# Second loop's front computed one round ahead; three convolution blocks split over ScalarE and GpSimd

## The chip, the cores and the metric

One core of one Trainium2 chip. The time is the device time of one launch in microseconds, the median of the runs shown. The kernel is written engine by engine: TensorE (PE), VectorE (DVE), ScalarE (ACT), GpSimd (POOL) and SyncE (SP, which issues the DMAs) each have an instruction stream of their own, in order, and meet only at semaphores.

## The reference

Two layers over 8 sequences of 512 tokens with 128 features. Layer 0 (attention and 32 experts) is the first loop and is not touched. Layer 1, for each sequence:

```python
xn = layernorm(x)                                  # the outer normalisation, eps 1e-5
z  = zrms(xn, w_ln1)                               # x * rsqrt(mean(x*x)) * (1 + w)
q, k, v, gate = split(z @ W_qkvz); b, a = split(z @ W_ba)
beta = sigmoid(b); g = -exp(A_log) * softplus(a + dt_bias)
q, k, v = split(silu(causal_dwconv(concat[q, k, v], conv_w)))   # 4 taps, each channel by itself
core = gated_delta_rule(l2norm(q), l2norm(k), v, g, beta)       # chunks of 128 tokens
h = xn + (rms(core) * silu(gate)) @ W_out;  x2 = zrms(h, w_ln2)
a1 = h + moe(x2; 8 experts of 64, top 2)
a2 = ffn(xn; 8 experts of 512, top 2, gelu, router xn @ w_router)
out = x + a1 + a2
```

## The kernel before

Both layers are hardware loops of 8 rounds (`Fori(0, LOOPS)`, one per engine), one round per sequence. The order of the work in a round of the second loop is written out by hand in `schedule_l1` (L132 to L175) as a list of steps; every engine walks through the same list and issues its own part of each step, so a step that stands earlier in the list is ahead of all later ones in the queue of each engine that has a part in it.

Each round of the second loop begins with a *front* that is not in the list and stands at the head of the loop's body. DVE: statistics of `x1` (L1189 to L1194), `xn1` (L1431), its mean square (`ms`, L1408 to L1411), `zz` (L1437), the router's shift (L1414, L1415), `zT` (L1441), then beta, the parts of the gate `sp` and the router's top 2 (L1445 to L1453). POOL: two powers (L1122, L1124). PE: `xn1` transposed (L654), the router's product (L665), `zz` transposed, the product with `Wba` (L674). ACT: the copy `xn1T` (L979), three exponentials (L981 to L985), a logarithm (L987). `x1` for the next round is loaded by SP late in the round before (L442).

After the front comes the convolution. Its 24 blocks of 128 channels go two at a time: `qkv` (PE, L682, block m into PSUM bank 2 + m % 4; ACT, L994, writes the last tap, block times weight, to `CV`), `taps` (DVE, L1478: three scaled additions per block, read from the bank, added into `CV`), `silu` (ACT, L1001). Blocks 0 to 7 are queries and keys and also go through a square (ACT, L1006) and a sum of squares on PE (`ssq`, L708, read by `stat`, DVE L1495); blocks 8 to 15 are values. Between the two halves lie the decay matrices `Gam` (scans on DVE L1490, ACT L1013, POOL L1137) and the products of keys (`prep`, PE L721, DVE L1521). The pieces of the last feed-forward (`ffn(n)`: `fh` on PE L859, gelu on ACT L1078, `fo` on PE L869) are strewn between the steps. After the values come `wfT` (DVE L1467), `cz` (PE L729, waits for `wfT` because it uses the same bank), the substitution (DVE L1534, L1536) and the chunks. The round ends with h1 to h5 (the second normalisation and the router of the small experts), `facc` 7 and the four pairs of small experts `moe1` (PE L909, L911, L915, L903; ACT L1089; DVE L1688, L1692) and the last addition `moe1_last` (DVE L1698), which raises `out_ready`.

The lines of the value half's order:

```python
order += [("scan", 1), ("gam",), ("prep", 0), ("prep", 1), ("qkv", 8), ("prep", 2), ("prep", 3), ("rr",), ("qkv", 10)]
order += [("taps", 8)] + ffn(2) + [("taps", 10)] + ffn(2) + [("silu", 8), ("qkv", 12), ("taps", 12), ("silu", 10), ("qkv", 14)]
order += [("taps", 14), ("silu", 12), ("wfT",), ("silu", 14), ("cz", 0), ("cz", 1), ("stat2",), ("cv", 0), ("sub", 0)]
```

## Time and profile before

| | |
|---|---|
| median of 3 runs | 3202.34 us (3197.88 to 3214.34) |
| the profiled execution | 3201.73 us, its span 3199.9 us |
| PE / DVE / ACT / POOL busy in the span | 2706.7 / 2034.1 / 1180.9 / 380.0 us |
| mean granted TensorE clock | 0.88 |
| chain that ended last | PE 52%, issue 27%, DVE 9%, DMA 4%, ACT 4% |

The second loop takes the last 2020 us of the span. In a timeline row the columns are start, busy time, engine, line, operation, output<-input, shapes and count; in brackets how long the engine was idle before it and for whom. Rows that merge several instructions give the time from the first to the last.

### The profile page before, as it was taken

What the parts mean: (1) busy time and instruction counts of PE and PEld (TensorE: products, weight loads), DVE (VectorE), ACT (ScalarE), POOL (GpSimd) and SP (SyncE); (2) the same over time, 40 slices, a digit from 0 to 9 for tenths busy, and PEclk for the clock granted to TensorE, in tenths of its full rate; (3) what the DMA queues carried; (4) which work ended last, traced back from release to release, by engine and by line L of the source; (5) the groups of instructions that cost most, each with busy time, mean ns of one, the idle gap of its engine ahead of it and who ended that gap; (6) DMA issues with size and microseconds to landing.
All of it is one profiled execution on the core that took longest, in us unless ns stands there. A gap on an engine that the chain in (4) does not pass through costs nothing.

```text
span 3199.9 us, 48490 instructions
## 1 busy us (share of the span) xinstructions
PE 2706.7 (85%) x14996; PEld 1821.9 (57%) x14996; DVE 2034.1 (64%) x6290; ACT 1180.9 (37%) x2164; POOL 380.0 (12%) x282
## 2 busy tenths in 40 slices
PE   2888888888888867987997997897898798798799
PEld 1434344343443425864874684685596495586487
DVE  4757567575665858458557657557656755845855
ACT  0132231322313234435444444444444444443543
POOL 0000000000000002112112112021120220211211
PEclk9888889898898967997997997997998899799799
DMA  4010201202012021101101101101201201110110
GB/s 137 9 37 11 27 17 21 37 7 32 13 26 37 2 50 53 34 28 40 47 11 57 47 11 53 51 8 47 60 1 54 53 8 40 41 34 28 47 40 14
DMA packets 133704, 109.69 MB, mean 34 GB/s; under 512 B 76968, under 2 KB 117488, under 8 KB 132944
## 3 DMA queue, kind: packets, MB, share of 16 engines
q1 hardware_dynamic: 130192, 100.01, 12.5%
q10 hardware_dynamic: 3264, 6.82, 0.6%
q8 instruction: 100, 1.64, 0.2%
q14 instruction: 148, 1.21, 0.1%
HBM read 86.62 MB, written 20.19 MB: 33 GB/s over the span
## 4 chain that ended last, share of the span: by engine, by line
PE 52%; issue 27%; DVE 9%; DMA 4%; ACT 4%; SPq 2%; POOL 2%; DVEq 0%; ACTq 0%; POOLq 0%
PE bank L859 5%; PE bank L869 4%; PE bank L654 4%; DMA arena<-scrk 3%; PE bank L708 2%; PE bank L729 2%; PE bank L553 2%; PE bank L608 2%; PE bank L811 2%; PE bank L769 2%; PE bank L774 2%; PE bank L757 2%; DVE arena L1478 2%; PE bank L761 2%; PE bank L682 2%
## 5 line engine op out<-in xcount | busy, mean ns | idle before, releaser
L869 PEld LDWEIGHTS bank<-wring,arena 128*128 128x128 f32 x2048 | 272.1, 194 | 118.8 <-issue 117.6
L859 PE MATMUL bank<-arena,wring 128*128 128x512 f32 x512 | 286.2, 641 | 41.2 <-ACT arena L1078 41.2
L1078 ACT ACTIVATE arena<-bank,w_b 128x512 f32<-128x512 f32 x256 | 175.9, 687 | 309.7 <-PE bank L859 309.4
L1478 DVE SCALAR_TENSOR_TENSOR arena<-bank,w_convw,arena 128x511 f32<-128x511 f32 (+2 forms) x384 | 255.1, 734 | 43.1 <-ACT arena L994 42.8
L869 PE MATMUL bank<-wring,arena 128*128 128x128 f32 x2048 | 274.0, 278 | 0.0
L960 ACT ACTIVATE arena<-bank 128x512 f32<-128x512 f32 x136 | 81.2, 597 | 501.3 <-PE bank L538 427.4
L1343 DVE CUSTOM_DVE_ANT_0 bank<-bank,arena 128x128 f32<-128x128 f32 (+3 forms) x512 | 248.9, 492 | 0.0
L969 ACT ACTIVATE arena<-bank 128x512 f32<-128x512 f32 (+1 forms) x384 | 171.1, 536 | 147.0 <-PE bank L595 145.5
L654 PE MATMUL bank<-w_ident,arena 128*128 128x128 f32 (+2 forms) x1032 | 147.6, 284 | 64.0 <-DVE arena L1431 62.1
L568 PE MATMUL bank<-arena 48*128 48x128 bf16 (+3 forms) x512 | 111.2, 319 | 69.0 <-DVE arena L1343 35.7
L1046 ACT ACTIVATE arena<-bank 128x512 f32<-128x512 f32 (+1 forms) x256 | 118.5, 487 | 135.5 <-PE bank L769 69.5
L654 PEld LDWEIGHTS bank<-w_ident,arena 128*128 128x128 f32 (+2 forms) x1032 | 121.2, 143 | 81.4 <-DVE arena L1431 63.8
L538 PE MATMUL bank<-arena 128*128 128x512 f32 x272 | 157.8, 664 | 7.8 <-ACT arena L960 7.8
L553 PE MATMUL bank<-arena 128*128 128x128 f32 x1088 | 161.8, 293 | 2.7 <-DVE arena L1328 2.7
L1643 DVE SCALAR_TENSOR_TENSOR arena<-bank,arena 128x128 f32<-128x128 f32 x224 | 63.0, 344 | 154.2 <-PE bank L869 152.4
L324 DVE TENSOR_TENSOR tick<-nhalf 128x1 f32<-128x1 f32 x597 | 93.2, 156 | 99.1 <-PE bank L568 92.5
L682 PE MATMUL bank<-arena,w_Wqkvz 128*128 128x512 f32 x256 | 151.4, 734 | 1.3 <-DVE arena L1478 1.3
L541 PE MATMUL bank<-arena 128*128 128x512 f32 x272 | 152.0, 643 | 0.0
L568 PEld LDWEIGHTS bank<-arena 48*128 48x128 bf16 x512 | 34.1, 93 | 204.6 <-DVE arena L1343 92.6
L553 PEld LDWEIGHTS bank<-arena 128*128 128x128 f32 x1088 | 135.7, 196 | 22.7 <-issue 11.7
L1147 POOL TENSOR_TENSOR arena<-arena,w_blk 128x512 f32<-128x512 f32 x64 | 79.7, 1266 | 555.8 <-PE bank L757 358.7
L729 PE MATMUL bank<-w_Wqkvz,arena 128*128 128x512 f32 x128 | 82.5, 794 | 61.7 <-DVE arena L1467 61.1
(275 smaller groups left out, 5271.5 us busy)
## 6 DMA issues: line engine op xcount, KB each, us to landing
wring<-in_w_last SPq DMA_DIRECT2D x64, 512.0 KB, 3.3
arena<-scrg SPq DMA_DIRECT2D x32, 512.0 KB, 5.4
arena<-scrq SPq DMA_DIRECT2D x108, 64.0 KB
arena<-scrk SPq DMA_DIRECT2D x108, 64.0 KB
scrn<-arena SPq DMA_DIRECT2D x64, 64.0 KB, 1.9
arena<-scrn SPq DMA_DIRECT2D x8, 512.0 KB, 3.5
scrx<-arena SPq DMA_DIRECT2D x8, 512.0 KB, 2.6
arena<-scrx SPq DMA_DIRECT2D x64, 64.0 KB, 2.1
```

The costliest lines, as they stand in the source:

```text
L538: mm(bk[:, :], W["gate0"][:, p, :] if p < PR0 else W["sg"][:], xnT, start=True, stop=True).then_inc(*s["p_gate"].up)
L541: mm(bk[:, :], W["up0"][:, p, :] if p < PR0 else W["su"][:], xnT, start=True, stop=True).then_inc(*s["p_up"].up)
L553: last = mm(bank[7][:, t * P:(t + 1) * P], HID[:, p % 2, t * P:(t + 1) * P], W["down0"][:, p, :] if p < PR0 else W["sd"][:], start=(p == 0 ...
L654: return nc.tensor.transpose(dst, src, W["ident"][0:k, 0:k])
L682: mm(bk[:, :], W["Wqkvz"][:, m * P:(m + 1) * P], zT, start=True, stop=True).then_inc(*s["p_qkv"].up)
L729: mm(bk[:, :], zT[:, c * P:(c + 1) * P], W["Wqkvz"][:, w:w + 4 * P], start=True, stop=True).then_inc(*s["p_z"].up)
L859: mm(bank[HBANK[e]][:, :], wring[:, e % 2, k * P:(k + 1) * P], xn1T, start=True, stop=True).then_inc(*s["p_fh"].up)
L869: last = mm(bank[OBANK[e]][:, t * P:(t + 1) * P], GH[:, f % 2, t * P:(t + 1) * P], wring[:, e % 2, FC * P + k * D:FC * P + (k + 1) * D], s ...
L969: fn(PT[:, slot, col:col + w], bank[SBANK[n % 4]][:, 0:w], ACT.Exp, scale=float(HD) ** -0.5).then_inc(*s["a_p"].up)
L1078: fn(GH[:, f % 2, :], bank[HBANK[f // FC]][:, :], ACT.Gelu_apprx_tanh, bias=W["b1"][:, f:f + 1]).then_inc(*s["a_gh"].up)
L1343: v.tensor_tensor_reduce(bk[:, 0:w], bk[:, 0:w], W["maskq"][:, S - w:S], 1.0, PAD, ALU.add, ALU.max, mx[:, col:col + 1]).then_inc(*s["v_ma ...
L1478: ins = v.scalar_tensor_tensor(out=cv[:, k:S], in0=bank[2 + m % 4][:, 0:S - k], scalar=W["convw"][:, m, 3 - k:4 - k], in1=cv[:, k:S], op0= ...
```

## The change

The front is taken out of the loop's head. One copy of it runs ahead of the loop for sequence 0 (`ahead_of_loop`); in the loop it becomes steps of the list that compute the next sequence's front: `gn` behind `h4`, `gx` behind `facc` 7, and `gT`, `gz`, `gr`, `gzT`, `gba`, `gend` among and behind the four `moe1`. Its PSUM results now all lie in bank 0. The last round computes a front that nobody reads. Three blocks of values (9, 11, 13) lose their three DVE taps: ACT writes block times weight into a buffer (`A[0]` or `A[1]` in turn) and POOL adds it into `CV`; the third of each block waits until POOL has freed the first buffer. Whoever waited for `v_cv` of such a block now waits for `g_tap` (`convolved`).

```diff
+POOLED = (9, 11, 13)
...
+def convolved(m):
+
+    return ("g_tap", 3 * POOLED.index(m) + 3) if m in POOLED else ("v_cv", m + 1 - sum(p < m for p in POOLED))
...
-    order += [("h2",), ("facc", 6), ("h3",)] + ffn(1) + [("h4",)] + ffn(2) + ffn_rest() + [("h5",), ("facc", 7)]
-    order += [("moe1", p) for p in range(PR1)] + [("moe1_last",)]
+    order += [("h2",), ("facc", 6), ("h3",)] + ffn(1) + [("h4",), ("gn",)] + ffn(2) + ffn_rest() + [("h5",), ("facc", 7), ("gx",)]
+    order += [("moe1", 0), ("gT",), ("gz",), ("moe1", 1), ("gr",), ("moe1", 2), ("gzT",), ("moe1", 3), ("gba",), ("moe1_last",), ("gend",)]
...
+            def gT(b, k):
+                if k:
+                    pe.wait_ge(*s["v_w96b"].at(b, 1))
+                for t in range(NT):
+                    pe.wait_ge(*s["v_xn1"].at(b, t + 1, k))
+                    last = tr(bank[0][:, t * P:(t + 1) * P], xn1[:, t, :])
+                last.then_inc(*s["p_xn1T"].up)
+
+            def gr(b, k):
+                pe.wait_ge(*s["a_xn1T"].at(b, 1, k))
+                for t in range(NT):
+                    last = mm(bank[0][:, t * EF:(t + 1) * EF], xn1T[:, t * P:(t + 1) * P], W["rf"][:], start=True, stop=True)
+                last.then_inc(*s["p_rf"].up)
+
+            def gzT(b, k):
+                pe.wait_ge(*s["v_lm"].at(b, 1, k))
+                for t in range(NT):
+                    pe.wait_ge(*s["v_z"].at(b, t + 1, k))
+                    last = tr(bank[0][:, t * P:(t + 1) * P], zz[:, t, :])
+                last.then_inc(*s["p_zT"].up)
+
+            def gba(b, k):
+                pe.wait_ge(*s["v_zT"].at(b, 1, k))
+                for t in range(NT):
+                    last = mm(bank[0][:, t * 16:(t + 1) * 16], zT[:, t * P:(t + 1) * P], W["Wba"][:], start=True, stop=True)
+                last.then_inc(*s["p_ba"].up)
+
+            ahead_of_loop(gT, gr, gzT, gba)
...
+                pe.wait_ge(*s["v_hid1"].at(b, 0))
                 pe.wait_ge(*s["v_zT"].at(b, 1))
...
+            def gend(b, k):
+                act.wait_ge(*s["v_lm"].at(b, 1, k))
+                fn(lf, lf, ACT.Exp).then_inc(*s["a_fe"].up)
+                act.wait_ge(*s["p_ba"].at(b, 1, k))
+                fn(ba, bank[0][:, 0:64].rearrange("p (t n) -> p t n", t=NT), ACT.Exp, scale=-1.0).then_inc(*s["a_eb"].up)
+                act.wait_ge(*s["v_ab"].at(b, 1, k))
+                fn(sp, sp, ACT.Exp, scale=-1.0).then_inc(*s["a_eab"].up)
+                act.wait_ge(*s["a_eab"].at(b, 1, k))
+                fn(sp, sp, ACT.Ln, bias=1.0).then_inc(*s["a_sp"].up)
...
+            ahead_of_loop(gT, gend)
             with act.Fori(0, LOOPS) as b:
+                act.wait_ge(*s["v_hid1"].at(b, 0))
...
+                def taps(m0):
+                    for m in (m0, m0 + 1):
+                        for k in (1, 2, 3) if m in POOLED else ():
+                            c = 3 * POOLED.index(m) + k - 1
+                            if c >= 2:
+                                act.wait_ge(*s["g_tap"].at(b, c - 1))
+                            fn(A[c % 2][:, 0:S - k], bank[2 + m % 4][:, 0:S - k], ACT.Copy, scale=W["convw"][:, m, 3 - k:4 - k]
+                               ).then_inc(*s["a_tap"].up)
...
+                def taps(m0):
+                    for m in (m0, m0 + 1):
+                        if m not in POOLED:
+                            continue
+                        cv = CV[:, m % 4, :]
+                        pool.wait_ge(*s["a_cv"].at(b, m + 1))
+                        for k in (1, 2, 3):
+                            c = 3 * POOLED.index(m) + k - 1
+                            pool.wait_ge(*s["a_tap"].at(b, c + 1))
+                            if k > 1:
+                                pool.wait_ge(*s["g_tap"].at(b, c))
+                            tt(cv[:, k:S], cv[:, k:S], A[c % 2][:, 0:S - k], ALU.add).then_inc(*s["g_tap"].up)
...
+            def gn(b, k):
+                dve.wait_ge(*s["d_x1"].at(b, 16 + 16 * k))
+                norm_stats(chain("v_glink", b, k), x1, stats, mv, var4[:, :], EPS0).then_inc(*s["v_var1"].up)
...
+            def gx(b, k):
+                dve.wait_ge(*s["g_rstd1"].at(b, 1, k))
                 for t in range(NT):
                     v.tensor_scalar(xn1[:, t, :], x1[:, t, :], mv[:, t, 0:1], rstd[:, t:t + 1], ALU.subtract, ALU.mult
                                     ).then_inc(*s["v_xn1"].up)
...
+            ahead_of_loop(gn, gx, gz, gr, gzT, gend)
...
+                    own, begun = [m for m in (m0, m0 + 1) if m not in POOLED], s["v_tap"].n
                     for k in (1, 2, 3):
-                        for m in (m0, m0 + 1):
+                        for j, m in enumerate(own):
                             if k == 1:
...
```

## Rows read from the trace of the kernel before

**Rows 1.** Timeline (columns above), seam between the sixth and the seventh round
```profile
2690.29 1.28 ACT L979 ACT_TABLE_LOAD   x1 [2.09 <-issue]
2691.18 0.69 DVE L1698 TENSOR_TENSOR arena<-arena,bank 128x512 f32<-128x512 f32 x1 [1.25 <-PE bank L903]
...
2694.23 0.87 DVE L1189 BATCH_NORM_STATS2 stats<-x 128x6 f32<-128x128 f32 x4 [2.36 <-issue]
...
2704.64 5.46 PE L682 MATMUL bank<-arena,w_Wqkvz 128*128 128x512 f32 x8
...
2705.09 0.19 DVE L1445 TENSOR_TENSOR arena<-bank,w_dtb 128x32 f32<-128x32 f32 x1 [2.24 <-ACT arena L983]
...
2708.58 4.02 DVE L1478 SCALAR_TENSOR_TENSOR arena<-bank,w_convw,arena 128x511 f32<-128x511 f32 x6
```

**Rows 2.** Timeline, the small experts at the end of the sixth round
```profile
2680.23 1.12 DVE L1643 SCALAR_TENSOR_TENSOR arena<-bank,arena 128x128 f32<-128x128 f32 x4
2680.25 0.39 PE L915 MATMUL bank<-W96b,w_sel 96*128 96x512 bf16 x1 [1.81 <-DVE W96b L1209]
...
2683.72 1.02 PE L909 MATMUL bank<-arena,w_ge 128*128 128x512 f32 x2
...
2686.55 1.02 PE L909 MATMUL bank<-arena,w_ge 128*128 128x512 f32 x2
...
2689.99 1.16 PE L903 MATMUL bank<-w_de,arena 128*128 128x128 f32 x8 [0.45 <-DVE arena L1692]
```

**Rows 3.** Timeline, prices of the front's pieces, at full clock where PE
```profile
2667.16 0.60 PE L654 MATMUL bank<-w_ident,arena 128*128 128x128 f32 x4
...
2669.35 0.96 PE L885 MATMUL bank<-w_r,arena 128*128 128x8 f32 x8
...
2696.91 1.11 DVE L1431 TENSOR_SCALAR arena<-x,mv,rstd 128x128 f32<-128x128 f32 x4 [1.12 <-POOL rstd L1122]
...
2699.28 1.01 POOL L1124 TENSOR_TENSOR arena<-arena,nhalf 128x4 f32<-128x4 f32 x1 [2.40 <-DVE arena L1411]
```

**Rows 4.** Stages: us, PE, PEld, DVE, ACT, POOL busy (count), granted clock, DMA, GB/s
```profile
2694.00:2695.00 1.00, 0.00 (x0) 0.00 (x0) 0.77 (x4) 0.00 (x0) 0.00 (x0) 0.79 0.96 336
...
2720.00:2724.00 4.00, 4.00 (x19) 3.65 (x18) 4.00 (x7) 3.14 (x6) 0.00 (x0) 0.50 0.71 283
```

**Rows 5.** Timeline, end of the query and key half
```profile
2715.50 1.84 PE L708 MATMUL bank<-w_ones,arena 128*128 128x1 f32 x16
...
2720.35 10.53 PE L708 MATMUL bank<-w_ones,arena 128*128 128x1 f32 x48
...
2726.01 4.55 DVE L1490 TENSOR_TENSOR_SCAN arena<-arena,w_floor 128x512 f32<-128x512 f32 x4
...
2730.92 0.19 DVE L1495 TENSOR_SCALAR arena<-bank 128x32 f32<-128x32 f32 x1 [0.37 <-PE bank L708]
```

**Rows 6.** Timeline, the value half from block 11's copy on
```profile
2752.80 0.69 ACT L994 ACTIVATE arena<-bank,w_convw 128x512 f32<-128x512 f32 x1 [0.17 <-PE bank L682]
...
2757.22 0.69 ACT L1078 ACTIVATE arena<-bank,w_b 128x512 f32<-128x512 f32 x1 [1.73 <-PE bank L859]
...
2760.12 0.69 ACT L1078 ACTIVATE arena<-bank,w_b 128x512 f32<-128x512 f32 x1 [2.21 <-PE bank L859]
...
2765.07 1.25 ACT L994 ACTIVATE arena<-bank,w_convw 128x512 f32<-128x512 f32 x2
...
2765.78 7.96 DVE L1478 SCALAR_TENSOR_TENSOR arena<-bank,w_convw,arena 128x511 f32<-128x511 f32 x12 [5.53 <-ACT arena L994]
...
2774.38 4.64 PE L729 MATMUL bank<-w_Wqkvz,arena 128*128 128x512 f32 x5 [7.64 <-DVE arena L1467]
```

**Rows 7.** Source lines: POOL's multiplications of 128x512, and the scan (min/median/max ns)
```profile
L1156 POOL TENSOR_TENSOR junk<-arena x64: 1038/1039/1040, 1322.9 to 3152.3; 128x512 f32<-128x512 f32 x64
...
L1137 POOL TENSOR_TENSOR arena<-arena x64: 1032/1416/1953, 1216.3 to 2997.6; 128x512 f32<-128x512 f32 x64
...
L1490 DVE TENSOR_TENSOR_SCAN arena<-arena,w_floor x64: 1185/1214/1997, 1210.4 to 2991.8; 128x512 f32<-128x512 f32 x64
```

More of the change, by code:

```diff
@@ L651, in after @@
                     return bank[i]
[L653 to L671 removed]
+                pe.wait_ge(*s["v_hid1"].at(b, 0))
                 pe.wait_ge(*s["v_zT"].at(b, 1))
[L673 to L675 removed]
                 def qkv(m0):
                     for m in (m0, m0 + 1):
[L679 to L681 removed]
+                        bk = after(*convolved(m - 4), 2 + m % 4) if m >= 4 else bank[2 + m % 4]
                         mm(bk[:, :], W["Wqkvz"][:, m * P:(m + 1) * P], zT, start=True, stop=True
@@ L1089, in moe1 @@
                     fn(SG1[:, p % 2, :], bank[1 + p % 2][:, :], ACT.Silu).then_inc(*s["a_sg1"].up)
-                steps = {"qkv": qkv, "silu": silu, "gam": gam, "cz": cz, "cv": cv, "inv": inv, "so1": so1, "sdl": sdl,
-                         "ct": ct, "fh": ffn, "h4": h4, "moe1": moe1}
+                steps = {"qkv": qkv, "taps": taps, "silu": silu, "gam": gam, "cz": cz, "cv": cv, "inv": inv, "so1": so1, "sdl": sdl,
+                         "ct": ct, "fh": ffn, "h4": h4, "moe1": moe1, "gT": lambda: gT(b, 1), "gend": lambda: gend(b, 1)}
                 for step in L1:
@@ L1164, in h1 @@
                     tt(rz, ssq, nhalf[:, 0:NT], ALU.pow).then_inc(*s["g_rz2"].up)
-                steps = {"rr": rr_, "gam": gam, "inv": inv, "nrm0": nrm0, "nrm1": nrm1, "h1": h1}
+                steps = {"rr": rr_, "taps": taps, "gam": gam, "inv": inv, "nrm0": nrm0, "nrm1": nrm1, "h1": h1,
+                         "gn": lambda: gn(b, 1), "gx": lambda: gx(b, 1)}
                 for step in L1:
@@ L1402, in _ @@
             v.memset(gT, NEG)
-            with dve.Fori(0, LOOPS) as b:
-                link = chain("v_link1", b, 0)
-                def ms(src, ready):
-                    for t in range(NT):
-                        last = v.tensor_tensor_reduce(junk[:, t, :], src[:, t, :], src[:, t, :], 1.0, 0.0, ALU.mult, ALU.add,
-                                                      ssq[:, t:t + 1])
-                    link(last)
-                    v.tensor_scalar(ssq, ssq, 1.0 / D, EPS1, ALU.mult, ALU.add).then_inc(*s[ready].up)
-                def softmax_shift(ps, src_ready, ready):
-                    link(v.tensor_reduce(red4, ps, AX, ALU.max))
-                    v.tensor_tensor(lf, ps, red4.unsqueeze(2).broadcast_to((P, NT, EF)), ALU.subtract
-                                    ).then_inc(*s[ready].up)
-                def softmax_end():
-                    link(v.tensor_reduce(red4, lf, AX, ALU.add))
-                    link(v.reciprocal(rec4, red4))
-                    link(v.tensor_tensor(pad8[:, :, 0:EF], lf, rec4.unsqueeze(2).broadcast_to((P, NT, EF)), ALU.mult),
-                         alone=True)
-                    pick(link, 2, top2, pad8, EF, mrf)
-                dve.wait_ge(*s["d_x1"].at(b, 16))
-                norm_stats(link, x1, stats, mv, var4[:, :], EPS0).then_inc(*s["v_var1"].up)
-                dve.wait_ge(*s["g_rstd1"].at(b, 1))
@@ new lines, in ms, with softmax_shift @@
+            def ms(link, src, ready):
+                for t in range(NT):
+                    last = v.tensor_tensor_reduce(junk[:, t, :], src[:, t, :], src[:, t, :], 1.0, 0.0, ALU.mult, ALU.add,
+                                                  ssq[:, t:t + 1])
+                link(last)
+                v.tensor_scalar(ssq, ssq, 1.0 / D, EPS1, ALU.mult, ALU.add).then_inc(*s[ready].up)
+            def softmax_shift(link, ps, ready):
+                link(v.tensor_reduce(red4, ps, AX, ALU.max))
+                v.tensor_tensor(lf, ps, red4.unsqueeze(2).broadcast_to((P, NT, EF)), ALU.subtract
+                                ).then_inc(*s[ready].up)
@@ L1450, in _ @@
                 v.tensor_scalar(aab, aab, 0.0, None, ALU.max)
-                dve.wait_ge(*s["a_fe"].at(b, 1))
-                softmax_end()
+                dve.wait_ge(*s["a_fe"].at(b, 1, k))
+                softmax_end(link)
                 v.tensor_tensor(wf, pad8[:, :, 0:EF], mrf[:, :, 0:EF], ALU.mult).then_inc(*s["v_wf"].up)
+            ahead_of_loop(gn, gx, gz, gr, gzT, gend)
+            with dve.Fori(0, LOOPS) as b:
+                link = chain("v_link1", b, 0)
                 def gc():
@@ L1475, in taps @@
                             else:
-                                dve.wait_ge(*s["v_tap"].at(b, 2 * m0 + 2 * (k - 2) + m - m0 + 1))
+                                dve.wait_ge(*s["v_tap"].at(b, begun + len(own) * (k - 2) + j + 1))
                             cv = CV[:, m % 4, :]
```

112 lines of the change are left out of this document (50 added, 62 removed).

## The prediction

> **What bounds the kernel now.** I read the second loop round by round in the timeline; the rounds repeat to 0.1 us, so one seam and one value half stand for all. Three stretches matter.
>
> The seam. The last addition of a round ends at 2691.87 (2691.18 plus 0.69). DVE begins the next front 2.36 us later, having waited for nothing, and ACT takes up its head 2.09 us after its last silu: that is the price of a loop's turn on these engines. The front is one chain through DVE, POOL, PE and ACT, and the first tap starts only at 2708.58, 16.7 us after the addition [rows 1]. PE meanwhile has a few small products only, at half clock.
>
> The query and key half. DVE adds taps without a gap, and PE runs beside it just in time: `stat` waits 0.37 us for the last sums of squares and starts at 2730.92, 39.05 us after the addition, while the scan in front of it had ended at 2730.56 [rows 1, 5]. Both engines end together here.
>
> The value half. The reader is to see who waits: DVE finishes blocks 8 to 11 and then stands 5.53 us for ACT's copy of block 12. ACT in its turn waits in the gelu chain for PE (1.73 and 2.21 us). Only blocks 12 to 15 run at DVE's pace, 7.96 us for twelve taps, and behind them `cz` waits on PE for `wfT`, idle for 7.64 us [rows 6].
>
> **Part 1, the front moved among the small experts: 8 rounds, +4.3 us each.** `gn` (1.56 us on DVE: from 2694.23 to 1.12 before 2696.91 [rows 1, 3]) falls between `h4` and `h5`, into DVE's wait for the gap-free PE of the last feed-forward; I price it at nothing, and if that cover were gone it would be 1.3 us a round. The `x1` it reads is loaded by SP behind `h1`, several steps earlier; were it late, DVE would wait in front of `gn`. From `facc` 7 on nothing covers it. `facc` 7 runs 2680.23 to 2681.35, `xn1` takes 1.11, and with its mean square DVE is busy 2.40 [rows 2, 3], so until 2683.7. PE, done with its first selection product at 2680.64, waits for `xn1` and ends the transposes at about 2682.8; the second gate starts at 2682.9. Its gate, up and selection take 2.0 us, then the down product needs both multiplications of pair 0, which DVE now makes at 2683.7 to 2685.1. Down 1.1 and router product 0.96 [rows 3]: the third gate starts at 2687.1 instead of 2683.72, +3.4. From there PE is back to back at 2.83 us a pair [rows 2] with two additions, 0.60 and 0.96 [rows 3], of which some 0.6 fall into the 0.45 us that the last down product had waited for DVE and into DVE's slack: +0.9. Sum +4.3, so the last addition ends at 2696.2. The POOL powers (1.01 each) lie under DVE's multiplications. Bounds: 3.1, if only PE's own work counted (0.60, 0.96, 0.60, 0.96), and 6.
>
> **Part 2, the seam: 7 of them, -6.8 us each.** Count from the last addition, T. DVE must still do `gend`, 3.5 us (2705.09 to 2708.58) and turn, 2.36: ready at T+6.0. ACT's logarithm ends at T+2.5 (0.65 to the second exponential, the load of a table 1.28, two short ACTIVATEs), the turn 2.09, T+4.6. The head of ACT's body carried a table load before its first copy in every round [rows 1]; I take one there again, 1.28, so the first tap copy ends at T+6.6 and the taps start. By DVE alone `stat` would come at T+6.6+3.96 (six taps), +0.45 (gate), +2.1 (PE, back to DVE), +12.0 (eighteen taps), +0.7, +4.55 (scans) = T+30.4.
>
> PE does not keep up with that. Before, the front's products and the first four blocks ran on PE nearly without a pause up to 2710 [rows 1], and the sums of squares behind them ran at full clock (1.84 us for 16 passes at 2715.5); from 2720 on it is granted half, and 48 passes take 10.53, 3.5 for 16 [rows 4, 5]. Now PE has only four blocks at the round's start, ends them near T+5 (its own turn taken as ACT's, 2.1, then eight passes) and then stands 6 us until DVE has made the gate at T+11. At the old seam the grant fell to half within 3.8 us of PE's last product (2691.2; the mean of 2694 to 2695 is 0.79) [rows 4]. So I take half clock: `gc` 1.7 (seven small passes, at 0.22 to 0.24 by the 48), two blocks 2.75 (the eight passes of four blocks took 5.46 [rows 1]), sums 3.5, two blocks 2.75, three sums 10.5: 21.2 us, T+32.3. Before it was T+39.05: -6.8. At full clock for the first part it would be the scans' T+30.4, a gain of 8.6.
>
> **Part 3, the first round: +5 us, the last: +0.5.** The front ahead of the loop is as long as before, plus 0.6 because `zz` can only be transposed once the router's result has left bank 0. Then the loops are entered (nothing shows the price; I take half a turn, 1.0, between 0 and 2.4), ACT loads its table (1.28), and the half clock costs its 1.5 to 3 as at the other seams. The last round's `gend` runs while the output is stored.
>
> **Part 4, blocks 9, 11 and 13: 8 rounds, +3.5 us each.** DVE loses nine taps of 0.66 (7.96 over 12) [rows 6], 6 us a round, but six of them lie in front of a wait of 5.53 and save nothing. ACT gains nine copies of about 0.65 (0.69 for the full block, 1.25 for two). In its queue they stand ahead of what the chain waits for. POOL's addition has no row; the nearest is its 128x512 multiplication without broadcast, 1.04 us; 1.42 is the median of one with a broadcast operand beside the scans, and 1.95 the worst of it [rows 7]. I take 1.04: DVE's taps read one operand from PSUM, unlike the scans. A block then costs ACT 0.66 + 0.62, a wait until the first addition is done (started at 0.73, done at 1.77), and 0.65: 2.5 us. Count from the end of block 11's copy, 2753.49. Block 9's copies push gelu 0 and 1 by 2.4. Block 11's stand where ACT waited 2.21, so gelu 2 goes from 2.2 to about 2.6 late, as do gelu 3, silu 8 and 9 and copies 12 and 13 (2.7). Block 13's push the rest to +5.2: the copy of block 14 ends at 19.7 (2773.2). From there DVE has six taps, 3.96: 2777.2, where it was 2773.74. That is +3.5, and `wfT`, `cz` and all behind are late by it, since PE was already waiting there. Bounds: 2.5 (POOL at 0.8 and ACT at 0.6) and 6 (POOL at 1.95).
>
> The scans stretched from 1.21 to 2.00 us beside POOL, and POOL's own multiplications to 1.95 [rows 7]; no row shows taps beside POOL. The Trainium skill, "SBUF — State Buffer", section "Who interferes with whom", says that GpSimd shares a pair of ports with VectorE and that both contend when a VectorE instruction has two inputs in SBUF, but not when it has one at most, as a tap has. By that rule the addition stays near 1.04; with contention as in the rows part 4 would be 7 to 22 us dearer over eight rounds, which is rival (c). The same skill, "GPSIMD Engine Reference", section 3.1, puts an fp32 addition of 2048 elements at 4497 ns, about twice VectorE's; scaled to 512 that is an estimate of 1.12 us, and the sum by it would be 1 to 2 us higher.
>
> **The sum.** 8 x 4.3 = +34; 7 x -6.8 = -48; first and last round +5.5; together -8. Blocks 8 x 3.5 = +28. So +20 on the profiled execution's 3201.73, which lies 0.6 below the median: 3222.
>
> **Rivals.** (a) *The copies hide*, and the kernel is faster. ACT's waits in front of two gelus of the value half (1.73, 2.21) are two thirds of the 6 us of copies, and DVE has three taps less in the last four blocks, 2.0 us: 8 x -2.0 - 8 = -24, 3178. Against it: ACT works in order, and two of the three groups stand where it did not wait. It decides at block 14's copy: if that ends within 16.3 us of block 11's (before 2769.8), blocks 12 to 15 are shorter than before. (b) *PE keeps full clock*: the seam gives 8.6 instead of 6.8 (-13) and the first round 2 less: 3207. For it: 3.5 us of dense work at the round's start; against: the 6 us wait behind it. (c) *POOL's additions stretch* beside DVE to 1.42 to 1.95: two waits of ACT per round and DVE's end come later by 0.8 to 2.7: +7 to +22, some 3238. For it, the scans' rows; against, the operand in PSUM. (d) *The head needs no table load*: 7 x 0.6 less at most, inside the range.
>
> **How the numbers follow.** Within 0.5% means 3186.3 to 3218.4, about what a measurement can tell. Forecast 0.52, own range 3208 to 3236, of which 0.38 is slower and 0.14 the same; (b) 0.13, same; (c) 0.13, slower; (a) 0.18, faster, and 0.04 for a seam gain at the upper bound with a small part 4. So faster 0.22, same 0.27, slower 0.51. The range over all, with some of (a) left out, is 3190 to 3242.
>
> **What would show it.** In the new trace: the last addition to the first tap 6 to 7 us, to `stat` 32 (30.4 in (b)); the small experts' stretch 4 us longer; clock 0.5 from `gc` on; the gelus of the value half 2.5 late, the copy of block 14 after 2773 counted from block 11's copy, PE's wait before `cz` over 10 us. Wrong would be: POOL additions far from 1.04, DVE without a wait in the value half, or a round shorter than 252.6 by more than 2 us.

## The result and the profile after

The changed kernel took 3218.64 us (median of 13 runs, 3202.96 to 3232.45) against 3206.47 for the kernel before beside it (13 runs, 3196.76 to 3219.78): ratio 1.004, 95% interval 1.0023 to 1.0058. It is slower, by 12.8 us as the ratio has it; whether by more than 0.5% the interval leaves open. A second comparison later gave 1.0044 (1.0024 to 1.0065). The kernel before took 3206 us in some of the comparisons of this document and 3195 or 3196 in the others, so every version is given as its ratio to the kernel before beside it. The profiled execution took 3220.11 us, its span 3218.3.

First the page's busy times and the head of its chain:

```profile
PE 2699.4 (84%) x15020; PEld 1814.4 (56%) x15020; DVE 2000.5 (62%) x6274; ACT 1223.7 (38%) x2242; POOL 464.6 (14%) x356
...
PE 56%; issue 21%; DVE 8%; POOL 5%; DMA 4%; ACT 4%; SPq 3%; DVEq 0%; ACTq 0%; POOLq 0%
```

DVE lost 33.6 us of work, ACT gained 42.8, POOL 84.6, and "issue", time on the chain in which an engine waited for nothing that the profile shows, fell from 27% to 21%. None of that says what the change is worth. The second loop has to be cut into stretches. I take the starts of three DVE instructions: the last addition of a round, `stat`, and the copy `wfT`. Sums over the rounds of one profiled execution, in us:

| stretch | before | after | difference |
|---|---|---|---|
| up to the first `stat` (first loop, and the first round's front) | 1215.3 | 1227.0 | +11.7 |
| of these, the last `x1` of the first loop to the first `stat` | 51.8 | 51.8 | 0 |
| first round, `stat` to `wfT` | 42.8 | 46.0 | +3.2 |
| last addition to the next `wfT`, 7 times | 576.4 | 536.5 | -39.9 |
| `wfT` to last addition, 8 times | 1361.8 | 1404.4 | +42.5 |
| behind the last addition | 3.5 | 4.4 | +0.9 |

The last four rows sum to +6.7. The +11.7 above them lie in a loop that the change does not touch. Most of its rounds take about 133, 136.5 or 140 us, in another mix in each profile, and from its first to its last addition it takes 935 to 962 us over the profiles of this case: 945 before, 957 and 944 in the two profiles of the changed kernel. The second of these had -5.2 in the first row and +14.9 in the second loop. So I put the timed +12.8 down to the second loop, where the two profiles have 7 and 15; with one or two profiles of each kernel that is an attribution and not shown.

From one last addition to the next it is 252.6 us before. After, it is 252.0 to 252.7 with one of 249.6 in the first profile, and 252.4 to 252.7 with one of 255.9 in the second. The one of 249.6 is 3.0 shorter, which the prediction had named as a sign of being wrong. What the seams gain, the rest of the round takes back; the first round has the loss without a seam's gain.

Two of the pieces come in two forms before the change already, which the prediction, with one seam and one value half for all, did not see. From the end of the last addition to `stat` it is 39.05 us in four seams and 41.7 in three, where all the sums of squares run at half clock. The last tap of the value half ends 20.25 us behind block 11's copy in five rounds and 18.74 in three. On average the seam went from 40.85 us (start to start) to 30.65, -10.2, and `stat` to `wfT` from 41.65 to 46.0, +4.35.

The seam between the sixth and the seventh round, in the timeline after [answering to rows 1 and 5]:

```profile
2708.55 0.69 DVE L1762 TENSOR_TENSOR arena<-arena,bank 128x512 f32<-128x512 f32 x1 [1.43 <-PE bank L915]
...
2710.98 5.39 PE L694 MATMUL bank<-arena,w_Wqkvz 128*128 128x512 f32 x8 [2.47 <-issue]
...
2713.13 0.69 ACT L1014 ACTIVATE arena<-bank,w_convw 128x512 f32<-128x512 f32 x1 [1.54 <-PE bank L694]
...
2716.29 4.03 DVE L1542 SCALAR_TENSOR_TENSOR arena<-bank,w_convw,arena 128x511 f32<-128x511 f32 x6 [3.56 <-ACT arena L1014]
...
2720.70 0.64 PE L702 MATMUL bank<-arena,w_upto 128*128 128x32 f32 x2 [4.33 <-DVE arena L1522]
...
2725.53 1.84 PE L718 MATMUL bank<-w_ones,arena 128*128 128x1 f32 x16
...
2731.83 3.20 PE L718 MATMUL bank<-w_ones,arena 128*128 128x1 f32 x16 [0.95 <-ACT arena L1036]
...
2735.76 3.57 PE L718 MATMUL bank<-w_ones,arena 128*128 128x1 f32 x16 [0.74 <-ACT arena L1036]
...
2739.37 0.19 DVE L1559 TENSOR_SCALAR arena<-bank 128x32 f32<-128x32 f32 x1 [0.37 <-PE bank L718]
```

With T = 2709.24, the end of the last addition: first tap at T+7.1 (DVE had been idle for 3.56 us; the row names ACT, but the copy that this tap reads had ended at 2713.82), `gc` at T+11.5, `stat` at T+30.1 instead of T+39.05. ACT has no table load at its head (it comes at 2717.12, before the first silu). Of four groups of sixteen sums of squares the first two ran in 1.84 us each and the others in 3.20 and 3.57. The stages of that seam show the clock [columns as in rows 4]:

```profile
2716.00:2720.00 4.00, 0.37 (x1) 0.00 (x0) 3.71 (x6) 2.51 (x4) 0.00 (x0) 0.83 0.02 6
2720.00:2724.00 4.00, 3.30 (x10) 2.27 (x11) 2.17 (x7) 2.00 (x4) 0.00 (x0) 0.50 0.02 4
2724.00:2728.00 4.00, 4.00 (x21) 2.75 (x20) 4.00 (x8) 2.95 (x6) 0.00 (x0) 0.82 0.68 207
2728.00:2732.00 4.00, 3.05 (x21) 2.31 (x19) 4.00 (x7) 3.76 (x7) 0.00 (x0) 1.00 0.86 317
2732.00:2736.00 4.00, 3.26 (x18) 3.18 (x18) 4.00 (x6) 2.37 (x5) 0.00 (x0) 0.53 0.00 0
```

PE stands 4.33 us before `gc`, and the grant is half (0.50, 1.2 GHz) in the stage behind it, then mostly and wholly full (0.82 and 1.00, 2.4 GHz), and near half again (0.53) from 2732 on.

The small experts in front of it, where `xn1` now comes between `facc` 7 and the second gate [answering to rows 2]:

```profile
2692.89 1.12 DVE L1707 SCALAR_TENSOR_TENSOR arena<-bank,arena 128x128 f32<-128x128 f32 x4
...
2693.93 1.11 DVE L1483 TENSOR_SCALAR arena<-x,mv,rstd 128x128 f32<-128x128 f32 x4
2694.33 1.25 PE L463 MATMUL bank<-w_ident,arena 128*128 128x128 f32 x4 [1.02 <-DVE arena L1483]
2695.37 1.91 PE L921 MATMUL bank<-arena,w_ge 128*128 128x512 f32 x2
...
2700.39 1.10 PE L921 MATMUL bank<-arena,w_ge 128*128 128x512 f32 x2
```

`facc` 7 to the last addition, start to start, was 10.96 us in every round and is 15.6 in the median one. The transposes took 1.25 (0.60 at full clock) and the gate 1.91 (1.02): PE waits 1.02 for `xn1` behind a longer wait for the selection, and the grant is half.

The value half from block 11's copy on [answering to rows 6 and 7]:

```profile
2760.61 0.69 ACT L1014 ACTIVATE arena<-bank,w_convw 128x512 f32<-128x512 f32 x1 [0.17 <-PE bank L694]
2761.19 1.26 ACT L1023 ACTIVATE arena<-bank,w_convw 128x511 f32<-128x511 f32 x2
2761.95 3.60 POOL L1175 TENSOR_TENSOR arena<-arena 128x511 f32<-128x511 f32 x3 [4.68 <-ACT arena L1023]
...
2765.99 1.71 PE L871 MATMUL bank<-arena,wring 128*128 128x512 f32 x2 [4.56 <-ACT arena L1110]
...
2776.61 2.32 DVE L1542 SCALAR_TENSOR_TENSOR arena<-bank,w_convw,arena 128x511 f32<-128x511 f32 x3 [11.89 <-ACT arena L1014]
...
2779.10 0.69 ACT L1023 ACTIVATE arena<-bank,w_convw 128x509 f32<-128x509 f32 x1 [0.80 <-POOL arena L1175]
...
2780.73 1.25 ACT L1014 ACTIVATE arena<-bank,w_convw 128x512 f32<-128x512 f32 x2
2781.43 4.03 DVE L1542 SCALAR_TENSOR_TENSOR arena<-bank,w_convw,arena 128x511 f32<-128x511 f32 x6 [2.51 <-ACT arena L1014]
...
2786.10 5.77 PE L739 MATMUL bank<-w_Wqkvz,arena 128*128 128x512 f32 x8 [8.53 <-DVE arena L1531]
```

DVE's wait for block 12's copy grew from 5.53 to 11.89 us, because the taps in front of it end 3.3 us sooner after block 11's copy and the copy of block 12 comes 3.0 us later. Counted from the end of block 11's copy, block 14's copy ends at +20.1 and the last tap at +24.2; in the round read before, the last tap ended at +20.25. Source lines, POOL's new additions and DVE's taps (min/median/max ns):

```profile
L1175 POOL TENSOR_TENSOR arena<-arena x72: 1083/1086/1271, 1249.7 to 3033.2; 128x511 f32<-128x511 f32 x24, 128x510 f32<-128x510 f32 x24, 128x509 f32<-128x509 f32 x24
...
L1542 DVE SCALAR_TENSOR_TENSOR arena<-bank,w_convw,arena x312: 724/740/751, 1204.6 to 3037.6; 128x511 f32<-128x511 f32 x52, 128x510 f32<-128x510 f32 x52, 128x509 f32<-128x509 f32 x52
```

### The profile page after: what moved, and what is told of

It is laid out like the page before. It is cut to its first block, busy times and chain, and to the rows that moved or that the text cites. A ratio compares the mean times of both kernels' runs of the same rounds, so it can differ in the third digit from the quotient of the medians.

```text
span 3218.3 us, 48939 instructions
## 1 busy us (share of the span) xinstructions
PE 2699.4 (84%) x15020; PEld 1814.4 (56%) x15020; DVE 2000.5 (62%) x6274; ACT 1223.7 (38%) x2242; POOL 464.6 (14%) x356
## 4 chain that ended last, share of the span: by engine, by line
PE 56%; issue 21%; DVE 8%; POOL 5%; DMA 4%; ACT 4%; SPq 3%; DVEq 0%; ACTq 0%; POOLq 0%
PE bank L871 7%; PE bank L881 6%; PE bank L463 4%; DMA arena<-scrk 4%; PE bank L821 2%; POOL arena L1188 2%; PE bank L559 2%; SPq L380 2%; PE bank L739 2%; DVE arena L1542 2%; PE bank L779 2%; PE bank L784 2%; PE bank L614 2%; PE bank L767 2%; PE bank L771 2%
## 5 line engine op out<-in xcount | busy, mean ns | idle before, releaser
L1542 DVE SCALAR_TENSOR_TENSOR arena<-bank,w_convw,arena 128x509 f32<-128x509 f32 (+2 forms) x312 | 212.6, 736 | 141.7 <-ACT arena L1014 136.5
L463 PE MATMUL bank<-w_ident,arena 128*128 128x128 f32 (+2 forms) x1164 | 175.8, 289 | 85.7 <-DVE arena L1289 35.6
L463 PEld LDWEIGHTS bank<-w_ident,arena 128*128 128x128 f32 (+2 forms) x1164 | 135.1, 140 | 113.9 <-issue 62.1
L544 PE MATMUL bank<-arena 128*128 128x512 f32 x272 | 160.1, 673 | 8.5 <-ACT arena L973 8.5
L1188 POOL TENSOR_TENSOR arena<-arena 128x512 f32<-128x512 f32 x64 | 92.3, 1474 | 331.4 <-DVE arena L1566 331.4
L871 PEld LDWEIGHTS bank<-arena,wring 128*128 128x128 f32 x512 | 79.7, 193 | 102.8 <-ACT arena L1110 81.8
```

Of the source, the lines that this page charges most:

```text
L463: return nc.tensor.transpose(dst, src, W["ident"][0:k, 0:k])
L544: mm(bk[:, :], W["gate0"][:, p, :] if p < PR0 else W["sg"][:], xnT, start=True, stop=True).then_inc(*s["p_gate"].up)
L871: mm(bank[HBANK[e]][:, :], wring[:, e % 2, k * P:(k + 1) * P], xn1T, start=True, stop=True).then_inc(*s["p_fh"].up)
L1188: tt(g4, g4, scale, ALU.mult).then_inc(*s["g_gam"].up)
L1542: ins = v.scalar_tensor_tensor(out=cv[:, k:S], in0=bank[2 + m % 4][:, 0:S - k], scalar=W["convw"][:, m, 3 - k:4 - k], in1=cv[:, k:S], op0= ...
```

## The experiments

### The two halves of the change, each alone

The rotation alone:

```diff
-POOLED = (9, 11, 13)
+POOLED = ()
```

> The changed kernel with no block on ScalarE and GpSimd (POOLED empty), so the rotated front alone. Theory: the two parts are separate; from the two traces the seam is 8.9 us shorter at 7 places, the stretch from cz to the last addition 5.2 longer in 8 rounds, the rest -4: the second loop 25 us shorter than before, ratio about 0.992; the value half as before, 20.9 us from block 11's copy to cz. Rival A: the front alone gives nothing (my forecast: -8, ratio 0.9975). Rival B: the rotated program makes the untouched first loop longer, as in the one profile of the changed kernel (11.7 us from its first to its last addition): then 0.996 and a first loop of 957 us against 945.

Measured: ratio 0.9954 (0.9932 to 0.9977). Its profile is of an execution whose eighth round took 852.7 us; only what lies before it can be read: 252.6 us from addition to addition, seams (last addition to `stat`, start to start) of 33.9. So the same kernel went a second time:

> The rotation alone (no block on GpSimd) a second time: its first profile was of a disturbed execution, and only its rounds 1 to 7 could be read. Theory: 0.994 to 0.997 of the kernel before, 3188 to 3200 us; seams of 33.9 us with the sums of squares at half clock (10.2 us for 48 passes), from stat to wfT 43 us, from wfT to the last addition 175.7 us, rounds of 252.6 us. Rival: the 33.9 us belonged to the disturbed execution; then the seams come as in the changed kernel, 30.8 us, and the rounds near 249.5.

Measured: 3173.84 us, ratio 0.9933 (0.991 to 0.9956). The rotation alone is faster by 15 to 21 us. But this profile has other rounds: 245.7 to 247.5 us, seams of 30.0 to 31.1. The rival held: 33.9 is not this kernel's seam, it is one of two forms. Nor was it the usual one: with an eighth round of 252.6 us the first execution would have taken 3210 us, and the ten that the ratio rests on took 3171 to 3203. The first form (T = 2699.2), then the second (T = 2664.15):

```profile
2700.84 3.69 PE L694 MATMUL bank<-arena,w_Wqkvz 128*128 128x512 f32 x8 [2.38 <-issue]
...
2710.52 0.64 PE L702 MATMUL bank<-arena,w_upto 128*128 128x32 f32 x2 [5.99 <-DVE arena L1522]
...
2722.26 10.24 PE L718 MATMUL bank<-w_ones,arena 128*128 128x1 f32 x48
...
2732.53 0.19 DVE L1559 TENSOR_SCALAR arena<-bank 128x32 f32<-128x32 f32 x1 [1.46 <-PE bank L718]
```

```profile
2666.22 5.39 PE L694 MATMUL bank<-arena,w_Wqkvz 128*128 128x512 f32 x8 [2.79 <-issue]
...
2675.49 0.41 PE L702 MATMUL bank<-arena,w_upto 128*128 128x32 f32 x2 [3.88 <-DVE arena L1522]
...
2683.20 1.84 PE L718 MATMUL bank<-w_ones,arena 128*128 128x1 f32 x16
...
2693.43 0.19 DVE L1559 TENSOR_SCALAR arena<-bank 128x32 f32<-128x32 f32 x1 [0.37 <-PE bank L718]
```

In the first seam the first blocks run at full clock (3.69 us), PE stands 5.99 before `gc`, and everything up to `stat` is at half: T+33.3. In the second they run mostly at half (5.39), they end later, the wait is 3.88, and the first half of the sums runs nearly all at full clock: T+29.3. It looks as if fast first blocks, by the longer wait behind them, cost the clock of the sums. The other seams do not bear that out. The six rotated kernels without filler have 56 seams in their eight profiles. Of the 27 whose first eight passes took 3.7 us, 18 have all sums at half clock and 9 have not, and the waits of the 18 are mostly the shorter ones (5.1 to 6.0 us against 5.9 to 6.5); of the 29 with slower first passes 3 have. One of the 9, from the kernel with block 9 on GpSimd, below (T = 2437.56, `stat` at T+30.4):

```profile
2439.69 3.69 PE L694 MATMUL bank<-arena,w_Wqkvz 128*128 128x512 f32 x8 [2.85 <-issue]
...
2449.26 0.63 PE L702 MATMUL bank<-arena,w_upto 128*128 128x32 f32 x2 [5.88 <-DVE arena L1522]
...
2458.03 1.84 PE L718 MATMUL bank<-w_ones,arena 128*128 128x1 f32 x16
...
2467.93 0.19 DVE L1559 TENSOR_SCALAR arena<-bank 128x32 f32<-128x32 f32 x1 [0.36 <-PE bank L718]
```

In the next seam of the same execution the first passes take 3.70, the wait is 5.59, and all the sums run at half (T+33.5). So the form goes with the clock of the sums, the all-half form is the commoner one behind fast first blocks, and what decides between the two is open.

The blocks alone:

```diff
 (the kernel before, its front where it was)
+POOLED = (9, 11, 13)
```

> The kernel before with blocks 9, 11 and 13 on ScalarE and GpSimd, the front where it was. Theory: ScalarE's queue delays cz by 3.9 us in each of 8 rounds, +31 us, ratio 1.010; additions of about 1.2 us. Rival (the copies hide): -16 us, 0.995. Rival: the delay comes only with the rotated front: 1.000. First loop 945 us if its length does not hang on the program, 957 if the new semaphores are what changed it.

Measured: 3258.33 us, ratio 1.0165 (1.0142 to 1.0187), +53 us. The direction is that of the theory, the size is not: rounds are 6.8 us longer, 5.0 of it from `stat` to `wfT`, 0.6 in the seam and 1.4 behind `wfT`. On top of the rotation the blocks cost 35 us (0.9933 to 1.0044) where both ran in one comparison, and 28 (0.9954 to 1.004) by two separate ones. The two halves of the change are not additive; what the other 18 to 25 us are was not followed up.

### One block at a time

```diff
-POOLED = ()
+POOLED = (13,)
```

> rot_only with block 13 alone on ScalarE and GpSimd. Theory (place in ScalarE's queue): blocks 9 and 11 put 2.7 us on the way to block 12's copy, block 13 puts 2.5 on the way to block 14's and takes 2.0 off VectorE: cz comes 1.0 later than in rot_only where three blocks make it 3.5, so +8 us over rot_only against the +28 of all three. Rival (the cost is in VectorE's and GpSimd's meeting or in a longer addition, the same for each block): a third, +9, cannot be told apart by the time; then the trace decides: block 14's copy 17.4 us after block 11's against 15.0 and 20.1.

Measured: 3177.35 us, ratio 0.9943 (0.992 to 0.9966), between the two values of the rotation alone, whose intervals are 7 us wide to either side: the time cannot tell whether block 13 on GpSimd costs 8 us or nothing. The trace has a small price. Block 14's copy ends at +15.8 or +17.3 behind block 11's, where it was +13.2 or +14.7 without (the two forms of the value half), so 2.6 us later, as the theory had it; with three taps less behind it the last tap is 0.9 us later, some 7 us over eight rounds.

```diff
-POOLED = ()
+POOLED = (9,)
```

> The rotation, and block 9 alone on ScalarE and GpSimd (blocks 11 and 13 on VectorE). Theory (ACT's queue in front of block 12's copy sets the value half): block 9's three copies and the wait for POOL push gelu 0 and 1 and all behind them by 2.4 us, of which a part falls into ACT's wait of 2.2 us for PE; nothing is saved after the wait of DVE for block 12, since block 9's taps lie before it. So +0.5 to +2.4 us a round, +4 to +19 us over the rotation alone, while block 13 alone had cost nothing. Rival (only the three together cost, by their number): block 9 alone is free too, within 4 us of the rotation alone. Shown by: the wait of DVE for block 12's copy, 6 us with none on GpSimd, 8 with block 9, 12 with all three.

In the same comparison, the changed kernel again:

> The changed kernel once more, so that the three others of this call stand beside it on the same chip. Expected: 1.002 to 1.006 of the kernel before, some 3219 us; its seams (last addition to stat, starts) near 30.8 us, its stretch from stat to wfT near 46 us, rounds of 252.5 or 249.3 us. If the seams came out at 34 us here, the half clock there would be chance of an execution and not a property of the kernel, and the comparison of seams between kernels would lose its meaning.

Measured: block 9 alone 3210.44 us, ratio 1.0045 (1.0019 to 1.007); all three 3209.47, 1.0044. Block 9 alone costs as much as the three together, 36 us on the rotation alone, more than either side expected. First the value half of the rotation alone, then with block 9:

```profile
2714.86 0.69 ACT L1014 ACTIVATE arena<-bank,w_convw 128x512 f32<-128x512 f32 x1 [0.17 <-PE bank L694]
2715.79 1.28 ACT L1110 ACT_TABLE_LOAD   x1 [0.24 <-PE bank L871]
...
2717.82 1.13 PE L871 MATMUL bank<-arena,wring 128*128 128x512 f32 x2 [2.14 <-ACT arena L1110]
...
2726.55 7.96 DVE L1542 SCALAR_TENSOR_TENSOR arena<-bank,w_convw,arena 128x511 f32<-128x511 f32 x12 [4.15 <-ACT arena L1014]
```

```profile
2745.45 0.69 ACT L1014 ACTIVATE arena<-bank,w_convw 128x512 f32<-128x512 f32 x1 [0.17 <-PE bank L694]
2746.04 1.25 ACT L1023 ACTIVATE arena<-bank,w_convw 128x511 f32<-128x511 f32 x2
...
2748.80 1.28 ACT L1110 ACT_TABLE_LOAD   x1
...
2750.83 2.07 PE L871 MATMUL bank<-arena,wring 128*128 128x512 f32 x2 [4.56 <-ACT arena L1110]
...
2761.57 7.96 DVE L1542 SCALAR_TENSOR_TENSOR arena<-bank,w_convw,arena 128x511 f32<-128x511 f32 x12 [10.29 <-ACT arena L1014]
```

From the end of block 11's copy (2715.55, 2746.14) the table load starts at +0.24 and at +2.66: the three copies of block 9, their wait for GpSimd included, are worth 2.4 us. DVE's taps start at +11.0 and +15.4: another 2.0 us between these two rounds. They come between the gelus, which followed each other with waits of 1.22 us and here with 2.16, 2.28 and 1.22, because PE's products take longer. But the rotation alone has such slow products by itself in some rounds: its taps start at +12.5 in three of eight rounds of this profile and in seven of eight of the other. With block 9 they start at +14.8 to +15.5 in all eight. So of the 2.0 us 1.2 are left against the mean of this profile, and 0.4 against the other's. The stages from 2750 and from 2754 with block 9, where those without it, from 2717 to 2723, are all at 1.00:

```profile
2750.00:2754.00 4.00, 3.17 (x9) 2.13 (x10) 1.28 (x2) 1.45 (x3) 0.39 (x1) 0.50 0.29 113
2754.00:2758.00 4.00, 4.00 (x19) 2.69 (x19) 0.00 (x0) 0.88 (x2) 0.00 (x0) 0.84 0.00 0
```

So block 9's copies cost twice: 2.4 us on ACT's queue, and 0.4 to 1.2 on the mean (2.0 in the rounds shown) in PE's clock, behind a wait of 4.56 us that had been 2.14. That this wait is what lowers the clock is read from rows, not shown by a run: before the change the stage 2756 to 2760 was granted 0.57 behind a wait of 1.92. Over the eight rounds `stat` to `wfT` sums to 362.5 us with block 9 and to 332.7 without, +30; the seams add 12, since three of seven are of the long form here (34.0 to 34.2, the others 30.3 to 31.1), and `wfT` to the last addition adds 6.5. That is more than the timed 36: the profiled execution of the rotation alone was the fastest of its six.

### The seam: loads, order, clock

DVE's turn was 2.36 us before and is 3.56 now. The output's store and two loads of weights start between the last addition and the first tap. The two loads were held back:

```diff
 (rotation alone; SyncE, before the loads of experts 0 and 1)
+sp_.wait_ge(*s["v_tap"].at(b, 1))
```

> As rot_only, and SyncE issues the first two loads of the last feed-forward's weights (1 MB) only after the first tap of the round. Theory: VectorE's turn of the loop takes 3.6 us in the rotated kernel against 2.4 before because these loads fall into it; with them later the turn is 2.4 again and the first tap comes 1 us sooner after the last addition, 7 x 1.0 = 7 us less than rot_only, as far as PE keeps up (the sums of squares end at the same time as the scans, so perhaps only half). Rival: the turn hangs on something else (what stands at the loop's head) and stays 3.6: same as rot_only.

Measured: 0.9976 (0.9959 to 0.9994), no better than 0.9954. The loads started at 2703.98, behind the first tap, and DVE's turn was 2.99 instead of 3.45. In all seven seams the first tap came at T+6.3 to T+6.5 instead of T+6.8 to T+6.9, and the seam went from 33.9 to 33.4 to 33.6. So the loads have a part in the turn, half of what was expected; `stat` still waited for the sums, all of them at half clock.

`xn1` later, so that the second gate does not wait behind it:

```diff
-("facc", 7), ("gx",)
-("moe1", 0), ("gT",), ("gz",), ("moe1", 1), ("gr",), ("moe1", 2), ("gzT",), ("moe1", 3), ("gba",), ...
+("facc", 7)
+("moe1", 0), ("gx",), ("moe1", 1), ("gT",), ("gz",), ("moe1", 2), ("gr",), ("moe1", 3), ("gzT",), ("gba",), ...
```

> As rot_only, with the step gx behind the first pair of small experts instead of ahead of it, and gT, gz, gr, gzT one pair later. Theory: PE no longer waits for xn1 behind facc 7 and keeps full clock there; the stretch from facc 7's start to the last addition is 14 to 15 us against 16.35 in the changed kernel and 11.64 before, 8 x 2 = 16 us less than rot_only. Rival: the chain of the front (transposes, router, gzT, zT, gba) now ends behind the last down product and gives it back: same as rot_only, or slower.

Measured: 3166.69 us, ratio 0.9876 (0.9854 to 0.9899). It beats the kernel before and both runs of the rotation alone. PE has the gate of pair 1 to do while DVE makes `xn1`, and the transposes and gates stay at full clock:

```profile
2667.72 1.13 DVE L1707 SCALAR_TENSOR_TENSOR arena<-bank,arena 128x128 f32<-128x128 f32 x4
...
2667.97 1.02 PE L921 MATMUL bank<-arena,w_ge 128*128 128x512 f32 x2
...
2671.21 0.60 PE L463 MATMUL bank<-w_ident,arena 128*128 128x128 f32 x4
...
2681.99 0.69 DVE L1762 TENSOR_TENSOR arena<-arena,bank 128x512 f32<-128x512 f32 x1 [2.14 <-PE bank L915]
```

`facc` 7 to the last addition is 14.3 us in every round, against 14.7 to 16.8 in the rotation alone: +3.3 on the kernel before, close to the 3.1 that PE's own added work comes to.

Products that nobody reads, to keep PE busy where it waits for the gate:

```diff
 (PE, behind qkv(2) of the order above)
+for _ in range(5): mm(bank[6][:, :], W["Wqkvz"][:, 0:P], zT, start=True, stop=True)
```

> rot_pair_later with five more products (block 0 of Wqkvz by zT, 512 columns, result into bank 6 and read by nobody) on PE behind the first four blocks of a round, where it otherwise waits for the gate. Theory: the granted clock stays at full through gc, blocks 4 and 5 and the sums of squares (in rot_only they ran at half: sums of 3.4 us for 16 passes, stat waited 1.46; in the changed kernel part at full: 1.84). Then stat comes when the scans end, 30.5 us after the last addition's start in every round, and PE is not late: 0 to 1 us a round less than rot_pair_later (30.1 to 30.6, once 34.5), and the 34 us form of the seam is gone. Rival: the products are just more work in PE's queue; at half clock they take 8.5 us and push gc by 2: a seam of 32 or more and a kernel 16 us slower.

The same, and eight more in front of `cz`:

> The same, and eight more such products into bank 1 behind the transposes of wf, where PE waited 7.6 to 8.5 us for wfT. Theory: cz then runs at full clock, 3.4 us for its eight passes instead of 5.8 to 6.4, and all behind it is 2 to 3 us earlier, 8 x 2.5 = 20 us less than pl_warm_seam. Rival: the rounds lock to the same lengths as before and it changes nothing, or the products are late themselves and delay cz.

Measured: 0.9882 (0.9861 to 0.9902) and 0.986 (0.9838 to 0.9882), against 0.9876 without any filler, which ran in another comparison. The first brings nothing that can be told. The second is the fastest version here (3147.16 us). The two ran side by side, five times each, and four of its five executions lie below all five of the first (3155.21); by the profiles `wfT` to the last addition is 7 us shorter in sum over the eight rounds, and the eight `cz` passes, from the first start to the last, take 3.2 us instead of 4.6 to 6.0. So the filler in front of `cz` brought some 8 us of the 20 expected. In the kernel before:

> The kernel before with the eight products behind the transposes of wf and nothing else. Theory: PE's clock alone is worth 2 to 3 us a round there: 20 us less, ratio 0.994, cz at full clock. Rival: no change; rounds stay at 252.6.

Measured: 1.0001 (0.9984 to 1.0017). The `cz` products ran at full clock (3.2 us instead of 5.9), and no time came of it. The seam's filler on the rotation alone:

> The rotation alone, and five products of 128x512 that nobody reads (into a bank free at that time) on PE behind the first four blocks of the round, where PE otherwise stands some 6 us until the gate is made. Theory (the seam is limited by the granted clock of the sums of squares): with the filler PE is granted full clock there, the seam goes from 33.9 to about 30.7 us, which DVE's scans then set, and the kernel gains 7 x 3.2 = 22 us on the rotation alone, at most; 3170 to 3180. Rival 1 (the filler, at half clock itself 3 us long or more, only delays PE): the clock stays at 0.5 and the seam is as long or longer; 3195 to 3215. Rival 2 (the clock is full, and what the seam gains is given back later in the round, where the grant then falls): seam 30.7, but rounds still of 252.6 us, no gain; 3195.

Measured: 0.9909 (0.9879 to 0.9938), against 0.9933 in the same comparison: inconclusive. All seams are of the short form, 30.0 to 30.3, six of them behind first passes of 3.7 us, and `gc` and the first sums run at full clock; but the rotation alone had 30.0 to 31.1 in this comparison by itself, and the rounds with filler are no shorter (245.8 to 249.2 against 245.7 to 247.5). The filler fixes the form of a seam that is often short without it, and what it brings is less than can be told here.

## Why the prediction was right, and which of its steps were not

The forecast was 3222 on 3202.34 shown, +20; the runs gave +12.8 and the second loop of two profiles +7 and +15. As a ratio the forecast is 1.006, just above the interval of the first comparison (1.0023 to 1.0058) and inside that of the second. By its parts, in us, with the two profiles of the changed kernel:

| term | forecast | measured |
|---|---|---|
| small experts, each | +4.3 | +4.65 (`facc` 7 to last addition) |
| `wfT` to last addition, 8 times | +34 | +43 and +46 |
| seam up to `stat`, each | -6.8 | -8.9 in the seam read, -10.2 and -9.8 on average |
| seam and value half, last addition to `wfT`, 7 times | -23 (7 x -3.3) | -40 and -36 |
| first round's front | +5 | 0 |
| last round | +0.5 | +0.9 |
| value half up to `wfT`, each | +3.5 | +3.9 in the round read, +4.35 and +4.6 on average |
| all blocks, on the rotation | +28 | +28 and +35 |
| rotation alone | -8 | -15 and -21 |

**Part 1** was right in mechanism and slightly low. The third gate came 4.0 us later where 3.4 was forecast, because the transposes and the second gate ran at half clock. With the clock kept it is 3.3, in the order with the later `gx`. Pricing `gn` at nothing was right: `wfT` to `facc` 7 took 159.3 us before and 159.0 to 159.6 in the rotation alone. The changed kernel has another 0.8 to 1.1 us a round there, not forecast. It comes with the three blocks, for the kernel before with the blocks alone has it too (160.1 to 160.5 in seven rounds of eight); why was not traced.

**Part 2** failed in two of its steps. "I take one there again" was wrong: ACT's head has no table load, rival (d). DVE's turn was 3.56, not 2.36, and this gave back what the missing load had saved, and the first tap came at T+7.1, forecast T+6.6; of the kernels here it lies between T+6.8 and T+7.7 wherever the front is rotated and the loads are not held back. The step that moved the sum is "So I take half clock". Half clock throughout gives T+33.3 (forecast T+32.3), as the first profile of the rotation alone shows; but thirteen of the changed kernel's fourteen seams are of the other form, T+29.3 to T+30.5, which is what rival (b) had (T+30.4). Rival (b) was given 0.13 as all or nothing. The runs show two forms, both of them in one kernel and in one execution; the forecast should have been a mean of the two, and the 39.05 that it started from is itself the shorter of two, so that the gain is 10.2 on average. Neither (b)'s reason, dense work at the round's start, nor the forecast's, the long wait behind it, decides the form: dense first blocks at full clock and waits of 5.9 us stand in seams of both forms.

**Part 3** was wrong for the first round. The last `x1` to the first `stat` took 51.8 us before and after; in the profiles of the other rotated kernels it took 48.7 to 55.3, on both sides of that, so no price of entering a loop can be read from them. Its +5 is as large as most of the 7 us by which the forecast's +20 exceeds the timed +12.8, but larger errors than that met each other, as the last paragraph says.

**Part 4** was right, and by its own steps: +20.1 for block 14's copy (19.7), +24.2 for the last tap (23.7), a wait of ACT for GpSimd of 0.80 per block, and gelus 2.6 to 3.0 us late (2.4 and 2.6). POOL's addition, without a row before, takes 1.09 (taken as 1.04; the estimate of 1.12 beside it was nearer), and neither the additions nor the taps stretched beside each other, so (c) is out. One sign failed: PE's wait before `cz` was to pass 10 us and is 8.53, because PE's own last products in front of it end 3.0 us later as well. The taps read one operand from PSUM; the trace has them at 0.74 (median) and at most 0.75 over all 312, those beside POOL included. That agrees with the rule of the Trainium skill, "SBUF — State Buffer", section "Who interferes with whom", by which such an instruction does not contend with GpSimd. The single blocks bear out the attribution too, block 13 at 2.6 on the queue and 0.9 at the last tap, block 9 at 2.4 on the queue. What it had not seen is that block 9 alone carries the whole price: in the round read of the changed kernel the same delay costs PE less clock (0.67 and 0.90 in the stages from 2765 and 2769), in the one with block 9 alone more (0.50 and 0.84). Rival (a), the copies hide, had its point at 16.3 us from block 11's copy to block 14's; it was 20.1.

By the first profile, -17 in the seven stretches up to `wfT`, +8 in the eight behind it and -5 in the first round make the 14 us between the forecast's +20 and its +6.7. The -17 hold two errors of opposite sign: the seams gained 3.4 us each more than forecast, 24 in all, and the seven value halves lost 1.0 each more, 7. By the timed runs the rotation was undersized by 7 to 13 us and the blocks were right or up to 7 too low. So that the sum came out within 8 us is in part luck. The sign rested on part 4, and the runs of single parts confirm it: the rotation is a gain that the three blocks take back.

## What to carry to other kernels

Work moved from one engine to another is not priced by the busy time it frees but by whose queue it stands in: three copies of 0.65 us cost 2.4 us in front of a gelu on which PE waited, and the same three copies for block 13 cost 0.9 at the last tap, since the taps that they save lie behind them. When a step is pulled into a dense stretch, put the other engines' next ready work between its producer and its consumer (here one pair of experts, 0.6 to 0.8% of the kernel). And bring one cheap part of a change to the chip alone before adding the next: here one part gained 0.5 to 0.7% and the other lost 0.9 to 1.1%.

## What the runs showed of the hardware that was not expected

- The same code comes in two forms of clock within one execution. In the kernel with block 9 alone on GpSimd, behind first passes of 3.69 us and a wait of 5.88 us, the first sums took 2.20 and 1.84 us per 16 in one seam (`stat` at T+30.4); behind 3.70 and a wait of 5.59 in the next, 48 sums took 10.24 (T+33.5). Neither the first passes nor the wait tells the form.
- Lengths of identical code fall into steps: second-loop rounds of 245.7, 249.2, 252.6, 256.0 and 259.4 us, 3.4 apart, are found again and again, with others between them; most first-loop rounds take 133.2, 136.5 or 139.8. The kernel before, the changed one and the first profile of the rotation alone all have 252.6, with seams of 39.7 to 42.4, 30.0 to 31.2 and 33.9 to 34.0. So a stretch that gets shorter need not shorten the round, and one profile shows one mix: the rotation alone had 252.6 in one and 246.7 on average in the other. What sets the steps is open.
- A loop's turn on DVE is no constant: 2.36 us before, 3.56 after, 3.45 in the rotation alone and 2.99 with two loads started later.
- GpSimd's fp32 addition of 128x511 to 128x509 took 1.09 us, and 1.26 to 1.27 for the first of each block, beside VectorE's taps or alone.
